# Three reorderings at the seam between attention and the feed-forward part: V's last transposes, one low part of W_ffn, one chunk of pair 2

## The chip, the cores and the metric

One core of one Trainium2 chip runs the whole kernel in one launch. The metric is device time in microseconds (us). The kernel before takes 1227.71 us, the median of 3 runs (1227.65 to 1227.83). The profiler took one further execution of its own, and all trace rows come from that one.

## The reference, cut to what matters

`x` is 32 sequences of 64 channels by 1024. A small network on `cond_128` mixes eight 64x64 matrices per sequence (`z` below), attention with 32 heads and a 10-row adapter prefix runs on the result, and its output projection is added to `x`. Then comes a grouped convolution of 9 taps, and a feed-forward layer (`W_base`, with a top-2 routed low-rank part) on its result.

```python
x = x + _L0_attn_ref(_L0_cond_ref(x, cond_128, ...), w_attn, w_proj, adapter_wte, gating)
x = x + _L0_ffn_ref(_L0_cond2_ref(x, cond_128, weight, c_weight, fside_S_0), W_base, b_base, W_router, A, B)
# in _L0_attn_ref:  y = softmax(q k^T / sqrt(hd), causal) v + gating * softmax(q ak^T / sqrt(C)) av;  return y w_proj^T
# in _L0_ffn_ref:   base = xf W_base^T + b_base;  logits = xf W_router^T;  lora = sum over the top 2 experts of w (xf A_e^T) B_e^T * 2
```

## The kernel before, in words

**Passes.** Every large product is made in three passes of a float32r high part and low part (high by high, high by low, low by high). ScalarE makes the high part by a copy, VectorE the low part by a subtraction, TensorE multiplies. So each weight and each activation must have gone through ScalarE and then VectorE before TensorE may use it.

**Attention stage.** The 2048 tokens stand as 4 units of 512 tokens, the 1024 columns as 8 groups of 128. The program goes through 32 units (g, u), numbered n. In `unit_step` TensorE projects K, Q and V of unit n (`project_qkv`, L803) and between these does the attention of unit n-1: scores (`attend_scores`, L755), V's transposes (`turn_values`, four transposes of vT into the PSUM bank bV, L810), the transposes of the probabilities (`attend_transposes`, L764 and L771) and the products with the values (`attend_values`, L780 and L786). ScalarE copies V out of PSUM (vT, L1060), and once it is transposed copies it into vbd (L1069, four copies).

**The seam.** The attention of the last unit, m = 31, has no projection of a further unit beside it. TensorE's program fills it with the first output projections: `project_out(p, c0, c1)` (L858) multiplies chunks c0 to c1 of the 8 chunks of pair p (2 sequences, 128 tokens); a chunk is three passes by two matmuls of 512 columns. Before its first chunk it waits for y_lo of pair p and, because all pairs accumulate into the same two banks bP, for x1_set of pair p-1, the residual of the pair before. `residual(p)` (L1209, VectorE) reads bP, adds x and writes x1.

VectorE's order there is a list written by hand (L1307 to L1320): the low part of y of pair 1 (`split_y(1)`, L1201), low parts of W_ffn (`wffn_lo(i)`, L1194, eight in all), residual(0), the softmax of unit 31 (L1148 to L1184), split_y(2), residual(1), `convolved(0)` (L1221 and L1227: the bias onto the convolution, then its low part clo), the rest of the low parts, the low part of the low-rank weights. ScalarE's order (L1076 to L1088) is unit 31's copies and exponentials, then split_y(1) (L1007), wffn_hi(0 to 3) (L1000), attend_exp(31), split_y(2), wffn_hi(4 to 6), attend_copies(31), y_copy(31), split_conv(0), wffn_hi(7). Here vbd's copies of unit 31 stand ahead of split_y(1), and they wait for V's transposes.

SyncE issues every transfer of the seam in one order: y and x of pair 0, W_ffn's blocks 0 and 1, y of pair 1; then (L682 to L694) W_ffn's blocks 2 to 6, y of pair 2, x1 of pair 0 to memory (`put_aside`), x of pair 1, and x1 back in eight strided pieces for the convolution (`spread`, L672). GpSimd makes x1b = x1 + bias (`add_bias`, L726); the first one waits for aprobs of unit 31, and residual(p+1) waits for x1b of pair p.

**Feed-forward stage.** For each of 16 pairs p (`pair_step`): the last layer of pair p (`last_layer`, L885, 8 chunks of 9 matmuls), some chunks of pair p+2's output projection, `turn_hidden` (L895, one transpose), some more chunks, `low_rank` (L905), `convolve(p+1)` (L870), and the remaining chunks. Beside these, VectorE does router(p) (L1241 to L1267), finish(p) (L1273, L1275), convolved(p+1) and residual(p+2). The chunk boundaries (c0, c1, c2) are (0, 3, 5) for all pairs but the first, where two chunks were already done after the first convolution.

Of the kernel before, what the change touches and what calls it, by code (L numbers as in the profile page):

```python
# [42 lines left out]
KC = L // P  # L43
# [20 lines left out]
def wait(eng, sem, value):  # L64

    if not isinstance(value, int) or value > 0:
        eng.wait_ge(sem, value)


def split_passes(hi_l, lo_l, hi_r, lo_r):  # L70

    return ((hi_l, hi_r), (hi_l, lo_r), (lo_l, hi_r))
# [286 lines left out]
def program(nc, d, psum, z, zbase, y_dram, x1_dram, ctx_dram, weights, out):  # L359
# [8 lines left out]
    with ExitStack() as ctx:  # L368
# [370 lines left out]
        def _(pe):  # L739
            mix_tensor(pe)  # L740
            def attend_scores(m, groups):

                pe.wait_ge(rotated[Q_], m + 1)
                pe.wait_ge(kbd_set, m + 1)
                wait(pe, aT_copied, m)
                wait(pe, pT_copied, 2 * m)
                wait(pe, ashifted, m)
                pe.wait_ge(akbd_set, groups)
                pe.wait_ge(avs_set, groups)
                for s in range(UP):  # L750
                    for b in range(2):
                        for t in range(2):
                            heads = slice(2 * HD * t, 2 * HD * (t + 1))
                            at = (s % 2) * SW
                            mm = pe.matmul(bS[2 * t + s // 2][NC * b:NC * b + NC, at:at + KW],  # L755
                                           qr[heads, (2 * s + b) * NC:(2 * s + b + 1) * NC],
                                           kbd[heads, 2 * s + b, :], start=True, stop=True)
                            if s == UP - 1 and b == 1:
                                mm.then_inc(scores, 1)
# [47 lines left out]
            def turn_values(m):  # L807
                pe.wait_ge(vT_copied, m + 1)
                for i in range(UP):
                    tr = pe.transpose(bV[:, i * P:(i + 1) * P], vT[:, i * P:(i + 1) * P], ident[:])  # L810
                tr.then_inc(v_tr, 1)
# [37 lines left out]
            def project_out(p, c0, c1):  # L849
                if c0 == 0:  # L850
                    pe.wait_ge(y_lo, p + 1)
                    wait(pe, x1_set, p)
                for c in range(c0, c1):
                    if p == 0:
                        pe.wait_ge(wp_lo, c + 1)
                    for i, (y, w) in enumerate(split_passes(*y_hi_lo[p], wphi, wplo)):
                        for n in range(2):
                            mm = pe.matmul(bP[:, n * 512:(n + 1) * 512], y[:, c, :], w[:, c, n * 512:(n + 1) * 512],  # L858
                                           start=(c == 0 and i == 0), stop=(c == KC - 1 and i == 2))
                if c1 == KC:  # L860
                    mm.then_inc(proj_mm, 1)

            def convolve(p):
                pe.wait_ge(x8_in, 16 * PH * (p + 1))
                wait(pe, conv_set, 2 * p)
                for b in range(2):
                    for g in range(CONV):
                        for j in range(2):
                            o = 512 * b + P * g
                            mm = pe.matmul(bC[:, o:o + P], x8[:, CONV * b + g, j:j + P], toep[:, g, j, :],  # L870
                                           start=(j == 0), stop=(j == 1))
                    mm.then_inc(conv_mm, 1)

            def last_layer(p, columns, c):

                if isinstance(p, int) and p == 0:
                    pe.wait_ge(wf_lo, c + 1)
                if c == 0:
                    pe.wait_ge(c_lo, 2 * (p + 1))
                for i, (a, w) in enumerate(split_passes(chi, clo, wfhi, wflo)):  # L880
                    for k in columns:
                        if c == 0 and i == 0:
                            wait(pe, bank_free[k], p)
                        at, n0, n1 = cuts[k]
                        mm = pe.matmul(bF[:, at:at + n1 - n0], a[:, c, :], w[c][:, n0:n1],  # L885
                                       start=(c == 0 and i == 0), stop=(c == KC - 1 and i == 2))
                        if c == KC - 1 and i == 2 and k == 2:
                            mm.then_inc(hidden_mm, 1)
                        if c == KC - 1 and i == 2 and k == 1:
                            mm.then_inc(ffn_mm, 1)  # L890

            def turn_hidden(p):
                pe.wait_ge(hw_set, p + 1)
                wait(pe, hwT_set, p)
                pe.transpose(bT[:, 0:P], hw[:], ident[:]).then_inc(hw_tr, 1)  # L895

            def low_rank(p):
                if isinstance(p, int) and p == 0:
                    pe.wait_ge(lora_lo, 1)
                pe.wait_ge(hwT_set, p + 1)  # L900
                for k in (2, 0, 1):
                    at, n0, n1 = cuts[k]
                    n1 = min(n1, L)
                    for h, w in split_passes(hwThi, hwTlo, loraBhi, loraBlo):
                        mm = pe.matmul(bF[:, at:at + n1 - n0], h[:], w[:, n0:n1],  # L905
                                       start=False, stop=True, skip_group_check=True)
                    if k != 0:
                        mm.then_inc(lora_mm, 1)
# [4 lines left out]
            m = NG * NU - 1  # L913
            pe.wait_ge(turned[Q_], NG * NU)
            pe.wait_ge(turned[K_], NG * NU)
            project_out(0, 0, KC)
            attend_scores(m, NG)
            turn_values(m)
            project_out(1, 0, 6)
            attend_transposes(m)  # L920
            project_out(1, 6, KC)
# [6 lines left out]
            def pair_step(p, ahead):  # L928
                if ahead >= 2:
                    for c in range(KC):  # L930
                        last_layer(p, (2, 0, 1), c)
                    c0, c1, c2 = (2, 5, 7) if p == 0 else (0, 3, 5)
                    project_out(p + 2, c0, c1)
                    if p == 0:
                        pe.wait_ge(y_copied, NG * NU)
                    turn_hidden(p)
                    project_out(p + 2, c1, c2)
                    low_rank(p)
                    convolve(p + 1)
                    project_out(p + 2, c2, KC)  # L940
                    return

                for k in (2, 0, 1):
                    if k == 1:
                        turn_hidden(p)
                    for c in range(KC):
                        last_layer(p, (k,), c)
                if ahead == 1:
                    convolve(p + 1)
                low_rank(p)  # L950

            for p in range(NP):
                pair_step(p, min(3, NP - 1 - p))
# [147 lines left out]
        def _(dve):  # L1101
# [90 lines left out]
            def wffn_lo(i):  # L1192
                dve.wait_ge(wf_hi_set, i + 1)
                dve.tensor_tensor(wflo[i][:], wf_raw[i][:], wfhi[i][:].bitcast(F32), ALU.subtract).then_inc(wf_lo, 1)  # L1194

            def split_y(p):
                dve.wait_ge(y_hi, p + 1)
                wait(dve, proj_mm, y_free(p))
                if p == 1:
                    dve.wait_ge(mm_done[V_], NU * NG)  # L1200
                dve.tensor_tensor(y_hi_lo[p][1][:], yst[:], y_hi_lo[p][0][:].bitcast(F32), ALU.subtract).then_inc(y_lo, 1)  # L1201
# [103 lines left out]
            for n in range(NG * NU):  # L1305
                unit_step(n // NU, n % NU)
            split_y(1)  # L1307
            for i in range(4):
                wffn_lo(i)
            residual(0)  # L1310
            attend_softmax(NG * NU - 1)
# [1 line left out]
            residual(1)  # L1313
            dve.wait_ge(fconsts, 16 * NFCONST)
            convolved(0)
            for i in range(4, KC):
                wffn_lo(i)
            dve.wait_ge(y_out, 16 * NG * NU)
            dve.wait_ge(lora_hi, 1)
# [113 lines left out]
```

## Time and profile before

| what | value |
|---|---|
| median of 3 runs | 1227.71 us |
| the profiled execution's own time | 1229.13 us |
| its span in the trace | 1226.6 us |
| PE busy | 1193.7 us (97%) |
| DVE busy | 736.8 us (60%) |
| ACT busy | 385.8 us (31%) |
| POOL busy | 79.2 us (6%) |
| share of PE in the chain that ended last | 93% |

PE is TensorE's matmuls, PEld its weight loads, DVE is VectorE, ACT ScalarE, POOL GpSimd, SPq SyncE's queue of transfers. Times in the trace are us from the span's start. In a timeline a row gives its start, its length, engine, line, operation, output and inputs, and the number of instructions; in brackets stands the engine's idle time before it and what ended that. Matmuls overlap, so the length of one is more than what it adds to the stream: the difference of two starts is what counts.

### The profile page before, as it was taken

To read this page: it belongs to the slowest core of one execution; us is meant where nothing else is said; L and a number is where in the kernel's file an instruction comes from. 1 tells how busy PE (TensorE), PEld (TensorE's weight loads), DVE (VectorE), ACT (ScalarE), POOL (GpSimd) and SP (SyncE) were. 2 spreads that over 40 slices of the span, in tenths; PEclk is the share of its full clock that TensorE was granted. 3 is DMA by queue.
4 is the path that set the end of the run, shared out by engine and by line. 5 is a ranking of instruction groups with operands and counts; after the bars stand their busy time and mean duration, and the time that the engine had idled before them with its cause. 6 is when DMAs were issued, how large, how long until landed. Compare 5 with 4: busy or idle time off the path is not lost.

```text
span 1226.6 us, 19491 instructions
## 1 busy us (share of the span) xinstructions
PE 1193.7 (97%) x7940; PEld 1036.6 (85%) x7940; DVE 736.8 (60%) x1489; ACT 385.8 (31%) x699; POOL 79.2 (6%) x41
## 2 busy tenths in 40 slices
PE   7899999999999999999999996999999999999998
PEld 6778888888888888888888885989999999999997
DVE  5966857767777768768577795533333333333332
ACT  4434443543535344344435462300100010110000
POOL 2700000000000000000000000100000111000001
PEclk9999999999999999999999998999999999999999
DMA  6311002001002002010020424422222232222221
GB/s 225 117 40 49 30 11 68 10 18 60 19 9 69 10 10 70 9 47 32 12 67 10 155 87 174 133 88 88 89 88 88 89 106 89 89 88 96 98 78 45
DMA packets 54917, 84.75 MB, mean 69 GB/s; under 512 B 5786, under 2 KB 41134, under 8 KB 53806
## 3 DMA queue, kind: packets, MB, share of 16 engines
q1 hardware_dynamic: 54830, 83.52, 20.2%
q8 instruction: 63, 1.03, 0.4%
q14 instruction: 24, 0.20, 0.1%
HBM read 58.33 MB, written 25.17 MB: 68 GB/s over the span
## 4 chain that ended last, share of the span: by engine, by line
PE 93%; DVE 4%; ACT 1%; issue 1%; DMA 0%; SPq 0%; DVEq 0%; ACTq 0%
PE psum L803 42%; PE psum L885 17%; PE psum L858 14%; PE psum L870 4%; PE psum L755 3%; PE psum L786 3%; PE psum L771 2%; PE psum L905 2%; PE psum L810 2%; DVE m_z L340 1%; DVE z L275 1%; PE psum L764 1%; PE psum L819 1%; PE psum L780 1%; DVE f_wflo L1194 0%
## 5 line engine op out<-in xcount | busy, mean ns | idle before, releaser
L803 PE MATMUL psum<-z,w_hi 128*128 128x512 f32 x1536 | 482.2, 395 | 3.6 <-DVE m_z L340 2.4
L803 PEld LDWEIGHTS psum<-z,w_hi 128*128 128x128 f32 x1536 | 283.7, 188 | 60.4 <-issue 2.6
L803 PE MATMUL psum<-z,w_lo 128*128 128x512 f32 x768 | 300.6, 391 | 0.0
L803 PEld LDWEIGHTS psum<-z,w_lo 128*128 128x128 f32 x768 | 144.5, 188 | 31.6
L1036 ACT ACTIVATE a_kbd<-a_kr 32x512 f32<-32x512 f32 x128 | 80.6, 630 | 225.5 <-DVE a_kr L1134 224.4
L726 POOL TENSOR_TENSOR f_x1b<-f_x,_bbase 128x1024 f32<-128x1024 f32 x16 | 49.3, 3079 | 1101.5 <-DVE a_aprob L1184 711.1
L885 PE MATMUL psum<-f_wfhi,f_chi 128*128 128x388 f32 (+1 forms) x384 | 94.5, 341 | 3.3 <-DVE f_clo L1227 1.8
L1148 DVE TENSOR_TENSOR a_prob<-psum,a_mask 128x512 f32<-128x512 f32 x64 | 44.0, 687 | 89.1 <-PE psum L755 89.1
L885 PE MATMUL psum<-f_wfhi,f_clo 128*128 128x388 f32 (+1 forms) x384 | 94.2, 340 | 0.0
L885 PE MATMUL psum<-f_wflo,f_chi 128*128 128x388 f32 (+1 forms) x384 | 94.2, 340 | 0.0
L1241 DVE COPY f_lg<-psum 128x8 f32<-128x8 f32 x16 | 2.7, 167 | 134.2 <-PE psum L885 134.2
L858 PE MATMUL psum<-f_wphi,f_yhi 128*128 128x512 f32 x240 | 77.1, 402 | 0.0
L858 PE MATMUL psum<-f_wplo,f_yhi 128*128 128x512 f32 x240 | 74.6, 392 | 0.0
L885 PEld LDWEIGHTS psum<-f_wfhi,f_chi 128*128 128x128 f32 x384 | 69.9, 189 | 5.3 <-DVE f_clo L1227 4.0
L858 PE MATMUL psum<-f_wphi,f_ylo 128*128 128x512 f32 x240 | 74.2, 390 | 0.0
L885 PEld LDWEIGHTS psum<-f_wfhi,f_clo 128*128 128x128 f32 x384 | 70.1, 189 | 0.0
L885 PEld LDWEIGHTS psum<-f_wflo,f_chi 128*128 128x128 f32 x384 | 69.8, 189 | 0.0
L1069 ACT ACTIVATE a_vbd<-psum 64x256 f32<-64x256 f32 x128 | 48.6, 380 | 45.7 <-PE psum L810 44.6
L1013 ACT ACTIVATE f_chi<-f_ct 128x512 fp32r<-128x512 f32 x32 | 20.2, 631 | 131.2 <-DVE f_ct L1221 131.2
L870 PE MATMUL psum<-_toep,_x 128*128 128x128 f32 x512 | 59.9, 275 | 0.0
L1018 ACT ACTIVATE f_rs<-f_rs 128x1 f32<-128x1 f32 x16 | 3.3, 203 | 179.1 <-DVE f_rs L1244 179.1
L870 PEld LDWEIGHTS psum<-_toep,_x 128*128 128x128 f32 x512 | 59.4, 192 | 0.1
(154 smaller groups left out, 1667.4 us busy)
## 6 DMA issues: line engine op xcount, KB each, us to landing
w_st<-in_wqkvT SPq DMA_DIRECT2D x8, 1536.0 KB, 7.2
m_x<-in_x SPq DMA_DIRECT2D x16, 512.0 KB, 4.3
y_scratch<-a_ysb SPq DMA_DIRECT2D x32, 256.0 KB, 2.5
f_yst<-y_scratch SPq DMA_DIRECT2D x16, 512.0 KB, 4.6
f_xt<-in_x SPq DMA_DIRECT2D x16, 512.0 KB, 3.9
x_scratch<-f_x SPq DMA_DIRECT2D x16, 512.0 KB, 2.6
_x<-x_scratch SPq DMA_DIRECT2D x128, 64.0 KB, 2.6
out<-f_osb SPq DMA_DIRECT2D x16, 512.0 KB, 2.7
```

The source lines that it names most:

```text
L726: pool.tensor_tensor(x1b[:].rearrange("p (m q) -> p q m", q=PH), x1[:].rearrange("p (q m) -> p q m", q=PH), bbase[:].rearrange("p (m q) -> ...
L755: mm = pe.matmul(bS[2 * t + s // 2][NC * b:NC * b + NC, at:at + KW], qr[heads, (2 * s + b) * NC:(2 * s + b + 1) * NC], kbd[heads, 2 * s + ...
L771: tr = pe.transpose(dst[:, j * P:(j + 1) * P], prob[t][:, 2 * j:2 * j + 2, :].rearrange("p h k -> p (h k)"), ident[:])
L786: mm = pe.matmul(y[2 * HD * hp:2 * HD * (hp + 1), (2 * s + b) * NC:(2 * s + b + 1) * NC], vbd[:, s, b, hp, :], pT[hp][:, s, NC * b:NC * b ...
L803: mm = pe.matmul(dst, w[:, c, x, :], zs, start=(c == 0 and i == 0), stop=(c == KC - 1 and i == 2))
L810: tr = pe.transpose(bV[:, i * P:(i + 1) * P], vT[:, i * P:(i + 1) * P], ident[:])
L858: mm = pe.matmul(bP[:, n * 512:(n + 1) * 512], y[:, c, :], w[:, c, n * 512:(n + 1) * 512], start=(c == 0 and i == 0), stop=(c == KC - 1 an ...
L870: mm = pe.matmul(bC[:, o:o + P], x8[:, CONV * b + g, j:j + P], toep[:, g, j, :], start=(j == 0), stop=(j == 1))
L885: mm = pe.matmul(bF[:, at:at + n1 - n0], a[:, c, :], w[c][:, n0:n1], start=(c == 0 and i == 0), stop=(c == KC - 1 and i == 2))
L1036: cp = act.activation(kbd[HD * h:HD * (h + 1), :, h % 2 * NC:(h % 2 + 1) * NC], kr[HD * h:HD * (h + 1), :].rearrange("p (b k) -> p b k", k ...
L1069: cp = act.activation(vbd[NC * h:NC * (h + 1), :, b, :, HD * h:HD * (h + 1)], bV[NC * b:NC * (b + 1), :].rearrange("p (s a h e) -> p s a h ...
L1148: dve.tensor_tensor(prob[t][:].rearrange("p (s h) k -> p s h k", h=2), score_slots[:, UP * t:UP * (t + 1), 0:2 * NC].rearrange("p s (h k) ...
```

## The change

Three edits of order; nothing is computed that was not computed before.

On TensorE, `turn_values(31)` goes ahead of `project_out(0, 0, KC)`; in the kernel before it stands behind both that and `attend_scores(31)`. On VectorE, three low parts of W_ffn instead of four go ahead of `residual(0)`, and the fourth (i = 3) goes to the head of those behind `convolved(0)`. On TensorE in pair 0, one of the two chunks of pair 2 that stood between `turn_hidden(0)` and `low_rank(0)` goes behind `convolve(1)`, where there was one chunk and are two now.

```diff
             pe.wait_ge(turned[K_], NG * NU)
+            turn_values(m)
             project_out(0, 0, KC)
             attend_scores(m, NG)
-            turn_values(m)
             project_out(1, 0, 6)
             attend_transposes(m)
             project_out(1, 6, KC)
...
-                    c0, c1, c2 = (2, 5, 7) if p == 0 else (0, 3, 5)
+                    c0, c1, c2 = (2, 5, 6) if p == 0 else (0, 3, 5)
                     project_out(p + 2, c0, c1)
...
             split_y(1)
-            for i in range(4):
+            for i in range(3):
                 wffn_lo(i)
             residual(0)
...
             convolved(0)
-            for i in range(4, KC):
+            for i in range(3, KC):
                 wffn_lo(i)
```

## Rows read from the trace of the kernel before

**Rows 1.** The page: TensorE's busy tenths in 40 slices of the span.
```profile
PE   7899999999999999999999996999999999999998
```

**Rows 2.** Waits of TensorE over the whole span (total, times, longest, us).
```profile
PE psum L858 <- DVE f_x L1209: 11.0, 1, 11.0
...
PE psum L885 <- DVE f_clo L1227: 1.8, 1, 1.8
```

**Rows 3.** The chain that ended last, 735 to 830 us (start, length, what).
```profile
739.01 11.11 PE psum L858 x48
...
751.28 0.60 PE psum L810 x4
...
760.90 1.82 DVE f_x L1209
```

**Rows 4.** Timeline of ScalarE: vT and vbd of unit 31.
```profile
737.73 0.60 ACT L1060 ACTIVATE a_vT<-psum 128x512 f32<-128x512 f32 x1 [1.57 <-PE psum L803]
...
751.91 1.55 ACT L1069 ACTIVATE a_vbd<-psum 64x256 f32<-64x256 f32 x4 [12.26 <-PE psum L810]
```

**Rows 5.** Timeline of VectorE at the seam.
```profile
755.71 5.19 DVE L1194 TENSOR_TENSOR f_wflo<-f_wf_raw,f_wfhi 128x1160 fp32r<-128x1160 f32 x4
...
772.14 0.24 DVE L1184 CAST a_aprob<-a_aprob 128x160 fp32r<-128x160 f32 x1
...
777.03 1.98 DVE L1209 TENSOR_TENSOR f_x<-psum,f_xt 128x1024 f32<-128x1024 f32 x1 [3.52 <-PE psum L858]
```

**Rows 6.** Timeline of TensorE at the seam.
```profile
762.85 1.19 PE L858 MATMUL psum<-f_wphi,f_yhi_next 128*128 128x512 f32 x2 [10.98 <-DVE f_x L1209]
...
772.72 0.60 PE L764 MATMUL psum<-_ident,a_aprob 128*128 128x128 f32 x4
```

**Rows 7.** Timeline of TensorE in pairs 0 and 1.
```profile
784.65 0.76 PE L885 MATMUL psum<-f_wfhi,f_chi 128*128 128x384 f32 x3
...
787.91 0.69 PE L885 MATMUL psum<-f_wfhi,f_chi 128*128 128x384 f32 x3
...
801.54 0.71 PE L858 MATMUL psum<-f_wphi,f_yhi 128*128 128x512 f32 x2
...
804.38 0.28 PE L905 MATMUL psum<-f_loraBhi,f_hwThi 128*128 128x248 f32 x1
...
812.67 0.80 PE L885 MATMUL psum<-f_wfhi,f_chi 128*128 128x384 f32 x3 [1.75 <-DVE f_clo L1227]
...
817.52 0.69 PE L885 MATMUL psum<-f_wfhi,f_chi 128*128 128x384 f32 x3
```

**Rows 8.** SyncE's queue and the landing of W_ffn's blocks (min, median, max).
```profile
740.09 3.05 SPq L614 DMA_DIRECT2D f_wf_raw<-in_wffnT  x5
...
DMA to landing us min/median/max: 4.2/6.5/9.3
```

**Rows 9.** Timeline of GpSimd: the first x1b.
```profile
772.46 4.08 POOL L726 TENSOR_TENSOR f_x1b<-f_x,_bbase 128x1024 f32<-128x1024 f32 x1 [711.13 <-DVE a_aprob L1184]
```

**Rows 10.** Timeline of VectorE: hwTlo of pair 0, and clo of pairs 1 and 2.
```profile
802.14 0.29 DVE L1267 TENSOR_TENSOR f_hwTlo<-psum,f_hwThi 128x128 fp32r<-128x128 f32 x1 [2.15 <-ACT f_hwThi L1021]
...
811.92 0.69 DVE L1227 TENSOR_TENSOR f_clo<-f_ct,f_chi 128x512 fp32r<-128x512 f32 x1 [0.70 <-ACT f_chi L1013]
...
841.56 0.69 DVE L1227 TENSOR_TENSOR f_clo<-f_ct,f_chi 128x512 fp32r<-128x512 f32 x1 [0.70 <-ACT f_chi L1013]
```

**Rows 11.** Stretches of 2 us: length, busy of PE, PEld, DVE, ACT, POOL, granted clock, DMA share, GB/s.
```profile
764.00:766.00 2.00, 2.00 (x7) 1.52 (x6) 1.96 (x3) 0.63 (x1) 0.00 (x0) 0.50 1.03 322
...
815.00:817.00 2.00, 2.00 (x8) 2.00 (x7) 0.58 (x1) 0.00 (x0) 0.00 (x0) 0.50 0.64 262
...
1208.00:1210.00 2.00, 1.94 (x11) 1.97 (x12) 0.79 (x1) 0.00 (x0) 1.07 (x1) 1.00 0.18 74
```

**Rows 12.** Timeline of TensorE: pair 2's last layer, and a wait near the end.
```profile
843.14 0.69 PE L885 MATMUL psum<-f_wfhi,f_chi 128*128 128x384 f32 x3
...
1208.06 0.41 PE L885 MATMUL psum<-f_wfhi,f_chi 128*128 128x384 f32 x1 [1.54 <-DVE f_osb L1273]
```

## The prediction

> **What bounds the kernel now.** I read the page's slices first: TensorE is busy at nine tenths or more nearly everywhere, and the one hole in the middle is the slice with a 6, at 736 to 767 us [rows 1]. So TensorE is the bound, and a change pays by what it takes out of TensorE's idle time or of its half-clock time. Second, the waits: one wait of 11.0 us of the first chunks of an output projection on the residual (DVE f_x L1209), and one of 1.8 us of the last layer on clo [rows 2]. Third, the chain and the timelines around the two, to see what ended last in each.
>
> At the first place, output projection 0 ends at 739.01 + 11.11 = 750.12, then the scores, then V's transposes, 0.60 long, at 751.28 [rows 3]. TensorE then has nothing until 762.85 [rows 6]. Pair 1's projection needs the banks that residual(0) frees, and residual(0) stands on VectorE behind split_y(1) and four low parts. split_y(1) needs ScalarE's high part, which stands behind vbd's copies, and these wait for V's transposes: vbd starts at 751.91 after 12.26 us of waiting [rows 4], the low parts start at 755.71 and take 5.19 [rows 5], and the residual runs from 760.90 for 1.82 [rows 3]. So in TensorE's order the transposes stand behind the very work whose end they hold up. The second place is 1.75 us at 812.67, where the last layer of pair 1 waits for clo [rows 7]; clo ends at 811.92 + 0.69 = 812.61 [rows 10].
>
> After each of the two the granted clock shows 0.50, the 1.2 GHz level: at 764 to 766 and at 815 to 817 [rows 11]. For the second its price can be read. The same six groups of three matmuls take 787.91 - 784.65 = 3.26 us in pair 0 and 817.52 - 812.67 = 4.85 in pair 1 [rows 7]: 1.59 us.
>
> **The change, part by part.**
>
> *V's transposes ahead.* They need vT, whose copy ends at 738.33 [rows 4], before TensorE is free at 739.01 [rows 3]; no wait is added. Four transposes are moved, no transfer with them. They put output projection 0 back by 0.60 us, so it ends at 750.72. ScalarE and VectorE then run vbd, split_y(1) and the low parts beside it. From vbd's start to the first low part's start was 755.71 - 751.91 = 3.80 us [rows 4, 5]; from about 739.7 that gives 743.5. Three low parts at 5.19 / 4 = 1.30 each [rows 5] end at 747.4 if their blocks have landed. That cover is output projection 0, and it has 3.3 us to spare.
>
> *Landing of W_ffn's blocks.* Block 2 is the first of five issued at 740.09, and landings take 4.2 to 9.3 us [rows 8]: between 744.3 and 749.4. In the worst case its high and low parts (1.3 us each, an estimate from the low part's row) end at 752.0 and residual(0) starts 1.3 us late. I take no delay, since the first of five should land nearer the short end, and keep 1.3 for the range. y of pair 2 is issued earlier too, behind these blocks; it is not needed until after unit 31's exponentials, 10 us on, and costs nothing.
>
> *One low part fewer ahead of residual(0).* By the sum above four would end at 748.7, still in time, so it is worth nothing alone, and 1.3 us only if block 3 is late. Behind convolved(0) it puts the four others and the low-rank low part back by 1.30. TensorE needs block 3 in the last layer's fourth chunk, three chunks (about 4.8 us) after its start at 784.65, while the low part of block 3 would be done 1.4 us after clo. Later blocks come every 1.3 us and are used every 1.6. Nothing.
>
> *What is late next.* Residual(0) starts at 750.76 and, at 1.90, ends at 752.66. TensorE starts pair 1 at about 752.8, where it was 762.85: 10.05 less. Its idle time there shrinks from 10.98 to about 0.9, because the scores end at 751.9. But unit 31's softmax still stands behind residual(0) on VectorE. It ended at 772.14 + 0.24 = 772.38 [rows 5], 9.66 after the residual's end at 762.72. So it will end at 752.66 + 9.66 = 762.32. TensorE needs six chunks before the transposes of the probabilities. At half clock at first it took 772.72 - 762.85 = 9.87 [rows 6]; at full clock a chunk is 1.38 (two chunks are 804.38 - 801.54 = 2.84, with some 0.09 of it a switch [rows 7]), six are 8.35, so it arrives at 761.2. A **new wait** of 1.2 us stands there, and the clock that is won back at this place is worth nothing. The transposes start at 762.4, where they were at 772.72: **10.3 us** in all.
>
> From there the order is as before. residual(1) waited for TensorE (3.52 idle), with x1b done at 772.46 + 4.08 = 776.54 and the residual started at 777.03 [rows 5, 9]; x1b hangs on the softmax like TensorE, so both move by about 10.3, and the half microsecond between them stays. spread(0) moves with residual(0) and stays ahead of the convolution.
>
> *The chunk of pair 2 behind the convolution.* low_rank(0) comes one chunk earlier: 804.38 - 1.38 = 803.0. It needs hwTlo, which ends at 802.43 [rows 10], 0.57 before; without that margin the gain would be cut by what is missing. The convolution, clo and the last layer of pair 1 follow it: clo at 812.61 - 1.38 = 811.23. TensorE now has two chunks (2.85) after a convolution ending at 809.28 - 1.38 = 807.9, so it arrives at 810.75 and waits 0.5 instead of 1.75. That is **1.38 us** saved in position (on top of the shift above).
>
> *The clock after it.* The trace has no wait of exactly 0.5 here. Bounds: the 1.75 us wait cost 1.59 more [rows 7], and a wait of 1.54 at 1208.06 [rows 12] was followed by a granted clock of 1.00 [rows 11]. 0.5 is nearer the latter, so I take the full **1.59 us** as saved, and 0 as the other end. The Trainium skill (TensorE: Matmul & The Clock Gate, the table under Why this matters for your kernels) gives a limit for idle gaps which a gap of 1.75 us does not reach. The trace disagrees, since the clock fell after just that gap. By the page the slow stretch would have another cause and stay, and the sum would be 1.59 less.
>
> **Sum:** 10.3 + 1.38 + 1.59 = 13.3 us. Against the profiled execution's 1229.13 that is 1215.8, a span of 1213.3. The profiled execution stands 1.42 above the median, and the same difference off the median gives 1227.71 - 13.3 = **1214.4**.
>
> **Rivals.**
> - *A: the clock falls at a new wait.* In the seam TensorE now waits twice, 0.9 and 1.2 us, and the second wait is followed by 1.2 us of transposes: 2.4 us without a full-width product, more than the 1.75 after which the clock fell. For it: that sum. Against: 1.54 held [rows 11, 12]. Price 1.59, on the path: 1216.0. The Trainium skill (same page, PE-mode transpose) says that transposes don't count as busy for the clock in the way matmuls do; by that this case is the one to expect. No row here separates it.
> - *B: the slow stretch in pair 1 stays,* by a phase of the clock rather than by the gap's length: 1216.0.
> - *C: block 2 lands late,* 1.3 us on residual(0) and all behind it: 1215.7.
> - *D: slower.* In pairs 2 to 13 TensorE reaches the last layer 0.9 us after clo (841.56 + 0.69 = 842.25 against 843.14 [rows 10, 12]). If the shift upset the order of VectorE and GpSimd there so that clo came more than 0.9 later, each pair would stall and might run at half clock. With the price of pair 1, up to 1.75 + 1.59 = 3.34 in each of 12 pairs, 40 us: 1254. It decides the sign at 1.1 us per pair. Against: what these pairs wait for is all relative to TensorE itself, and nothing in them is edited.
> - *E: the moved transposes don't free split_y(1),* because y of pair 1 or something else was late too. Then only the low part moved away (1.3) and the chunk (2.97) count: 1223.4. Against: ScalarE's 12.26 us are put down to the transposes, and nothing idles between vbd and the low parts.
>
> **How the numbers follow.** The forecast has 0.6, A 0.14, B 0.10, C 0.08, E 0.04, D 0.02, and 0.02 is left for others. The range reaches below by 1.4 for errors of the terms and of the comparison with the median, and above to A and C or A and B together (1217.6). 0.2% is 2.5 us, about what a measurement of this kernel can tell from no change. All but D and the rest lie more than that below 1227.7: faster 0.97, same 0.01, slower 0.02.
>
> **What would show it.** Right: TensorE's L858 wait on f_x drops from 11.0 to about 0.9; vbd starts near 739.7; a new wait of about 1.2 on a_aprob before L764 at about 762.4; pair 1's wait on clo at 0.5; clock 1.00 throughout the seam. Wrong: low parts idling for wfhi beyond 750.7 (C), a clock of 0.50 after 762 (A) or in pair 1's last layer (B), waits on clo in pairs 2 to 13 (D), ScalarE idle behind vbd (E).

## The result, and the profile after

| | before | after |
|---|---|---|
| median | 1227.77 us (1227.65 to 1228.57, 4 runs) | 1215.65 us (1215.03 to 1215.94, 4 runs) |
| ratio | | 0.9899, 95% interval 0.9882 to 0.9916 |
| profiled execution, its span | 1229.13, 1226.6 | 1215.03, 1212.7 |

The change takes 12.1 us off, 1.0%. The forecast was 1214.4 in a range of 1213.0 to 1217.6. The interval of the ratio reaches from 10.3 to 14.5 us off, so the times alone do not tell 12.1 from the 13.3 of the sum; what follows on the single terms rests on the traces. The slice that read 6 in TensorE's row [rows 1] reads 9 now:

```profile
PE   7899999999999999999999999999999999999998
```

The waits of TensorE over the whole span of the changed kernel (total, times, longest):

```profile
PE psum L764 <- DVE a_aprob L1184: 1.0, 1, 1.0
PE psum L858 <- DVE f_x L1209: 0.9, 1, 0.9
...
PE psum L885 <- DVE f_clo L1227: 0.4, 1, 0.4
```

The 11.0 us have become 0.9 and the 1.8 have become 0.4 [rows 2], and a wait that was not there before, 1.0 on aprob, has come in. The timeline of TensorE in the changed kernel puts them in order:

```profile
737.30 1.15 PE L786 MATMUL psum<-a_pT,a_vbd 128*64 128x64 f32 x32
738.38 0.66 PE L810 MATMUL psum<-_ident,a_vT 128*128 128x128 f32 x4
...
752.07 0.70 PE L858 MATMUL psum<-f_wphi,f_yhi_next 128*128 128x512 f32 x2 [0.94 <-DVE f_x L1209]
...
761.63 0.66 PE L764 MATMUL psum<-_ident,a_aprob 128*128 128x128 f32 x4 [1.00 <-DVE a_aprob L1184]
...
791.96 0.28 PE L905 MATMUL psum<-f_loraBhi,f_hwThi 128*128 128x248 f32 x1
...
800.32 0.79 PE L885 MATMUL psum<-f_wfhi,f_chi 128*128 128x384 f32 x3 [0.44 <-DVE f_clo L1227]
```

V's transposes now stand directly behind the products with the values. ScalarE no longer waits 12 us for them, and VectorE, which began the residual 10.78 us after the end of projection 0 (760.90 against 750.12 [rows 3]), is now idle 3.20 us before it. Here are ScalarE's and then VectorE's timeline of the changed kernel:

```profile
739.07 1.55 ACT L1069 ACTIVATE a_vbd<-psum 64x256 f32<-64x256 f32 x4
```

```profile
742.88 3.91 DVE L1194 TENSOR_TENSOR f_wflo<-f_wf_raw,f_wfhi 128x1160 fp32r<-128x1160 f32 x3
750.00 1.92 DVE L1209 TENSOR_TENSOR f_x<-psum,f_xt 128x1024 f32<-128x1024 f32 x1 [3.20 <-PE psum L858]
...
761.34 0.24 DVE L1184 CAST a_aprob<-a_aprob 128x160 fp32r<-128x160 f32 x1
```

The residual starts when projection 0 ends. The softmax ends 761.58 - 751.92 = 9.66 us after the residual, as it did before, and TensorE is there 1.00 us too early. The granted clock stays at 1.00 behind each of the three waits, on f_x, on aprob and on clo, as three stretches of 2 us of the changed kernel show (same columns as [rows 11]):

```profile
752.00:754.00 2.00, 1.93 (x9) 1.62 (x10) 1.93 (x4) 0.08 (x1) 0.00 (x0) 1.00 0.67 242
...
762.00:764.00 2.00, 2.00 (x16) 1.82 (x15) 0.71 (x1) 1.58 (x3) 2.00 (x1) 1.00 0.00 0
...
801.00:803.00 2.00, 2.00 (x13) 2.00 (x12) 2.00 (x2) 0.04 (x1) 0.00 (x0) 1.00 0.00 0
```

One thing has to be taken out before spans are compared. The start of unit 30's products with the values (L786), the last work ahead of all edits, lay between 736.94 and 738.22 us in the executions profiled for this study. That is scatter of an unedited part. So below stands, beside the times, **the stretch**: from that start to the end of the span. It is 1226.6 - 737.85 = 488.75 us in the first profile of before (its L786 row is in the experiment on the kernel before) and 1212.7 - 737.30 = 475.40 after: 13.35 less, where the sum said 13.3. Spans are given to 0.1 us, so a stretch is no finer than that.

### The profile page after: what moved, and what is told of

It reads as the page before. It is cut to its first block, busy times and chain, and to the rows that moved or that the text cites. A ratio compares the mean times of both kernels' runs of the same rounds, so it can differ in the third digit from the quotient of the medians.

```text
span 1212.7 us, 19491 instructions
## 1 busy us (share of the span) xinstructions
PE 1191.8 (98%) x7940; PEld 1034.2 (85%) x7940; DVE 736.6 (61%) x1489; ACT 386.0 (32%) x699; POOL 79.1 (7%) x41
## 4 chain that ended last, share of the span: by engine, by line
PE 93%; DVE 5%; ACT 1%; issue 1%; DMA 0%; SPq 0%; DVEq 0%; ACTq 0%
PE psum L803 42%; PE psum L885 17%; PE psum L858 14%; PE psum L870 4%; PE psum L755 3%; PE psum L786 3%; PE psum L771 2%; PE psum L905 2%; PE psum L810 2%; DVE m_z L340 1%; DVE z L275 1%; PE psum L764 1%; PE psum L819 1%; PE psum L780 1%; PE psum L205 0%
```

## The experiments

The first four put single parts of the change on the kernel before. All ran on one chip, beside 21 runs of before with a median of 1228.17 (1227.00 to 1229.42).

**V's transposes alone.**

```diff
+            turn_values(m)
             project_out(0, 0, KC)
             attend_scores(m, NG)
-            turn_values(m)
```

> V's transposes ahead of output projection 0, and nothing else of the change. Theory (the transposes alone held up the seam, and the softmax of unit 31 is late next): residual(0) starts when output projection 0 ends, since four low parts end before it too; 10.3 us less than the kernel before, about 1217.4. The wait on clo in pair 1 stays at 1.75 and the clock falls behind it. Rival (the low part taken away is needed as well): residual(0) starts about 1.3 us after projection 0's end, 9.0 us less, about 1218.7.

Measured: 1217.01 (1216.73 to 1217.29), ratio 0.9911 (0.9896 to 0.9926), stretch 476.67. TensorE's timeline of this run:

```profile
752.39 0.70 PE L858 MATMUL psum<-f_wphi,f_yhi_next 128*128 128x512 f32 x2 [0.94 <-DVE f_x L1209]
...
801.93 0.79 PE L885 MATMUL psum<-f_wfhi,f_chi 128*128 128x384 f32 x3 [1.72 <-DVE f_clo L1227]
...
805.22 0.69 PE L885 MATMUL psum<-f_wfhi,f_chi 128*128 128x384 f32 x3
```

The theory holds: the wait is 0.94 with four low parts too. But one thing came out otherwise. Behind the wait of 1.72 on clo the first six groups of the last layer take 805.22 - 801.93 = 3.29 us, the full-speed price. The clock did not fall, against the expectation.

**The low part alone.**

```diff
-            for i in range(4):
+            for i in range(3):
                 wffn_lo(i)
...
-            for i in range(4, KC):
+            for i in range(3, KC):
                 wffn_lo(i)
```

> Three low parts of W_ffn instead of four ahead of residual(0), and nothing else of the change. Theory (VectorE's list is the path of the seam once the transposes are late): residual(0) starts 1.3 us earlier, TensorE's wait on it falls from 11.0 to 9.7, 1.3 us less in all, about 1226.4. Rival (the low parts are beside the path, ScalarE's copies carry it): no change, 1227.7.

Measured: 1226.84 (1226.12 to 1227.48, 11 runs), ratio 0.9990 (0.9981 to 0.9999), which is 1.3 us. Its timeline of TensorE:

```profile
761.15 1.19 PE L858 MATMUL psum<-f_wphi,f_yhi_next 128*128 128x512 f32 x2 [9.70 <-DVE f_x L1209]
...
771.47 0.60 PE L764 MATMUL psum<-_ident,a_aprob 128*128 128x128 f32 x4
...
811.40 0.80 PE L885 MATMUL psum<-f_wfhi,f_chi 128*128 128x384 f32 x3 [1.74 <-DVE f_clo L1227]
```

The wait went from 10.98 to 9.70: while the transposes are late, the low part taken away was on the path. The rival is out. Here too the clock did not fall behind the wait of 1.74: the six groups of the last layer behind it ran at a granted clock of 1.00.

**The chunk alone.**

```diff
-                    c0, c1, c2 = (2, 5, 7) if p == 0 else (0, 3, 5)
+                    c0, c1, c2 = (2, 5, 6) if p == 0 else (0, 3, 5)
```

> One chunk of pair 2 behind the convolution, and nothing else of the change. Theory (position 1.38, and the granted clock no longer falls, 1.59): the wait on clo in pair 1 falls from 1.75 to about 0.4, the granted clock stays at 1.00 there, 3.0 us less in all, about 1224.8. Rival (the clock's fall has another cause): a granted clock of 0.50 stays in pair 1's last layer, 1.4 us less, about 1226.3.

Measured: 1226.64 (1225.48 to 1227.28, 11 runs), ratio 0.9989 (0.9980 to 0.9998): 1.5 us less, half of what the theory wanted, and yet not by the rival's mechanism. Its timeline of TensorE:

```profile
762.69 1.19 PE L858 MATMUL psum<-f_wphi,f_yhi_next 128*128 128x512 f32 x2 [10.97 <-DVE f_x L1209]
...
773.42 0.60 PE L764 MATMUL psum<-_ident,a_aprob 128*128 128x128 f32 x4
...
811.97 0.79 PE L885 MATMUL psum<-f_wfhi,f_chi 128*128 128x384 f32 x3 [0.35 <-DVE f_clo L1227]
...
815.26 0.69 PE L885 MATMUL psum<-f_wfhi,f_chi 128*128 128x384 f32 x3
```

The wait on clo is 0.35 and the six groups behind it take 3.29 us at full speed, as the theory wants. What is odd lies at the first place: the six chunks of pair 1 behind the 11 us wait took 773.42 - 762.69 = 10.73 us, where the first profile of before had 9.87 [rows 6]. So the time at half clock varied between executions, and the theory's base was one of them. The stretch bears this out: it is 1224.3 - 737.70 = 486.60, which is 2.15 below the first profile of before, and 3.01 below it once the 0.86 more at the first place is taken out.

**The change without its edit on VectorE.**

```diff
-            for i in range(3):
+            for i in range(4):
                 wffn_lo(i)
...
-            for i in range(3, KC):
+            for i in range(4, KC):
                 wffn_lo(i)
```

> The change without its edit on VectorE: four low parts ahead of residual(0). Theory (hidden behind output projection 0): the fourth low part ends about 1.9 us before projection 0 does, TensorE's wait on f_x stays at 0.9, the time is that of the change within its scatter, 13.3 us below before. Rival (needed once the transposes are early): 1.3 us more than the change.

Measured: 1215.34 (1214.73 to 1215.62), ratio 0.9897 (0.9882 to 0.9912), stretch 475.38 against 475.40 of the change. VectorE's timeline of this run shows the cover:

```profile
742.91 5.30 DVE L1194 TENSOR_TENSOR f_wflo<-f_wf_raw,f_wfhi 128x1160 fp32r<-128x1160 f32 x4
750.02 1.92 DVE L1209 TENSOR_TENSOR f_x<-psum,f_xt 128x1024 f32<-128x1024 f32 x1 [1.80 <-PE psum L858]
```

Even with the fourth low part VectorE is idle 1.80 us before the residual. The edit is worth 1.3 us alone and nothing beside the transposes.

**The kernel before, twice more.** No edit; this is the run that the odd rows asked for.

> The kernel before, unedited, for a second profiled execution. In the first the granted clock fell to 0.50 behind the wait of 1.75 in pair 1; in the runs with one part of the change alone it did not fall behind a wait of 1.72 and of 1.74. Theory (a wait of that length brings the clock down in some executions and not in others, so the 1.59 is counted in full only against the one profiled execution): the wait is 1.7 to 1.8 again, and the last layer's first six groups take either 3.3 or about 4.9 us. Rival (the fall belongs to the kernel before and is there in each execution): 4.9 here and in the next.

> The kernel before, unedited, for a third profiled execution; as the one before it. By the theory at least one of the two shows 3.3 us for the six groups and a granted clock of 1.00 there; by the rival neither does. The time of TensorE's six chunks of pair 1 behind the 11 us wait, 9.87 in the first profile and 10.73 in the run with the chunk alone, should vary as well, between about 9.7 and 10.7.

Measured: 1228.93 and 1226.78, each a single profiled execution. For comparison, the row of the first profile of before from which its stretch is counted:

```profile
737.85 1.15 PE L786 MATMUL psum<-a_pT,a_vbd 128*64 128x64 f32 x32
```

The timeline of TensorE in the second execution of before, then in the third:

```profile
737.69 1.15 PE L786 MATMUL psum<-a_pT,a_vbd 128*64 128x64 f32 x32
...
812.56 0.79 PE L885 MATMUL psum<-f_wfhi,f_chi 128*128 128x384 f32 x3 [1.81 <-DVE f_clo L1227]
...
817.38 0.69 PE L885 MATMUL psum<-f_wfhi,f_chi 128*128 128x384 f32 x3
```

```profile
737.23 1.15 PE L786 MATMUL psum<-a_pT,a_vbd 128*64 128x64 f32 x32
...
762.22 1.19 PE L858 MATMUL psum<-f_wphi,f_yhi_next 128*128 128x512 f32 x2 [10.98 <-DVE f_x L1209]
...
771.98 0.60 PE L764 MATMUL psum<-_ident,a_aprob 128*128 128x128 f32 x4
...
811.89 0.80 PE L885 MATMUL psum<-f_wfhi,f_chi 128*128 128x384 f32 x3 [1.74 <-DVE f_clo L1227]
...
815.18 0.69 PE L885 MATMUL psum<-f_wfhi,f_chi 128*128 128x384 f32 x3
```

A stretch of 2 us behind that wait, in the second and in the third execution:

```profile
814.00:816.00 2.00, 2.00 (x7) 2.00 (x7) 1.45 (x2) 0.00 (x0) 0.00 (x0) 0.50 0.39 158
```

```profile
813.00:815.00 2.00, 2.00 (x13) 2.00 (x12) 1.81 (x2) 0.00 (x0) 0.00 (x0) 1.00 0.22 88
```

The same program and the same wait: six groups in 4.82 us where the granted clock shows 0.50, and in 3.29 us where it stays at 1.00. The stretches are 1226.5 - 737.69 = 488.81 and 1224.3 - 737.23 = 487.07. So the 1.59 us belong to some executions of before and not to others; the rival, a fall in each, is out. How many have it is not shown. Nine runs of before on the same chip lie at 1228.27 to 1229.51, all nearer the second execution than the third, so there the fall may well be the common case.

The rest are edits of the changed kernel. The first three of them ran beside one more measurement of the changed kernel itself, on another chip than the runs above.

**The change once more.** No edit.

> The changed kernel once more, unedited, as the measure for the three beside it. By the forecast 13.3 us below before (1214.4); by the first measurement 12.1 (1215.65). Theory (the difference of 1.2 is scatter of the unedited first 60 us, where the clock falls in some phase): TensorE reaches the last unit's products with the values (L786) at a time that varies by up to 1 us between executions, and the stretch from there to the end is 13.3 us shorter than before. Rival (the clock falls at a new wait in some executions): the stretch from there to the end itself is longer by about 1.6 in this one.

Measured: 1215.43 (1215.37 to 1215.65), ratio 0.9896 (0.9881 to 0.9911), stretch 1213.0 - 737.62 = 475.38. The stretch is the same as in the first profile, 475.40, and the granted clock is 1.00 behind both new waits in each, so the rival did not come. Against before's 488.75 the theory's 13.3 holds, against the 487.07 of the third execution it is 11.7. So the 1.2 us that this expectation puts down to the opening can also be before's own scatter at half clock; no run splits them between the two.

**No chunk behind the convolution.**

```diff
-                    c0, c1, c2 = (2, 5, 6) if p == 0 else (0, 3, 5)
+                    c0, c1, c2 = (2, 5, 8) if p == 0 else (0, 3, 5)
...
-                    project_out(p + 2, c2, KC)
+                    if c2 < KC:
+                        project_out(p + 2, c2, KC)
```

> The changed kernel with no chunk of pair 2 behind the convolution: both stand between the transpose and the low-rank product of pair 0. Theory (a long enough wait brings the clock to half): the wait on clo in pair 1 grows from 0.44 by two chunks plus what low_rank(0) is later, to about 3.2; the last layer of pair 1 starts 2.8 us later than in the changed kernel, and the granted clock falls behind it, some 1.6 us more: 4.4 us above the changed kernel. Rival (the clock's fall in the kernel before was not due to the wait): 2.8 us above.

Measured: 1219.88 (1219.76 to 1220.04), 4.45 above the changed kernel, stretch 1217.5 - 737.93 = 479.57, 4.2 above. Its timeline of TensorE:

```profile
803.54 0.79 PE L885 MATMUL psum<-f_wfhi,f_chi 128*128 128x384 f32 x3 [3.07 <-DVE f_clo L1228]
...
808.36 0.69 PE L885 MATMUL psum<-f_wfhi,f_chi 128*128 128x384 f32 x3
```

Behind a wait of 3.07 the six groups take 4.82 us. All five runs lie within 0.3 us, so the fall probably came in each of them. The theory's two terms are both there: the last layer of pair 1 starts 65.61 us after L786 instead of 63.02, which is 2.6 (2.8 expected), and the six groups take 1.5 more (1.6 expected).

**Three chunks behind the convolution.**

```diff
-                    c0, c1, c2 = (2, 5, 6) if p == 0 else (0, 3, 5)
+                    c0, c1, c2 = (2, 4, 5) if p == 0 else (0, 3, 5)
```

> The changed kernel with pair 0's transpose of hw one chunk earlier, and three chunks of pair 2 behind the convolution instead of two. Theory (the wait on clo, 0.44, is all that is left there): low_rank(0) starts 1.38 earlier, clo with it, TensorE has three chunks of cover, no wait, 0.4 us less than the changed kernel. Rival (hw or hwTlo is late, one chunk is too little cover for it): TensorE waits up to 1 us at the transpose or at low_rank(0) and nothing is won, or up to 0.6 is lost.

Measured: 1215.14 (1214.66 to 1215.40), 0.3 below the changed kernel, with ranges that touch; stretch 1212.9 - 738.22 = 474.68, 0.7 below. The wait on clo is gone and none has come at the transpose or at the low-rank product. The theory's 0.4 lies between the two.

**Both waits filled.**

```diff
-            project_out(1, 0, 6)
+            project_out(1, 0, 7)
             attend_transposes(m)
-            project_out(1, 6, KC)
+            project_out(1, 7, KC)
...
-                    c0, c1, c2 = (2, 5, 6) if p == 0 else (0, 3, 5)
+                    c0, c1, c2 = (2, 4, 5) if p == 0 else (0, 3, 5)
```

> As the run with three chunks behind the convolution, and seven chunks of pair 1 instead of six ahead of unit 31's transposes of the probabilities. Theory (TensorE waits 1.0 us there for the softmax with work at hand that it could do): the wait disappears, the transposes start 0.4 later, and one chunk stands behind them instead of two; 1.0 us less there, 1.4 less than the changed kernel. Rival (with one chunk as cover, ScalarE's copies of the transposed probabilities, 1.7 us, become late): up to 0.5 of it comes back as a wait before the products with the values.

Measured: 1213.81 (1212.70 to 1214.04), ratio 0.9883 (0.9868 to 0.9898), 1.6 below the changed kernel beside it, with no overlap of the two ranges; stretch 1210.4 - 736.94 = 473.46, 1.9 below. This is the lowest median of all. Its timeline of TensorE, and then of VectorE:

```profile
761.50 0.60 PE L764 MATMUL psum<-_ident,a_aprob 128*128 128x128 f32 x4
...
764.53 1.15 PE L786 MATMUL psum<-a_pT,a_vbd 128*64 128x64 f32 x32
```

```profile
765.48 1.96 DVE L1209 TENSOR_TENSOR f_x<-psum,f_xt 128x1024 f32<-128x1024 f32 x1 [3.13 <-POOL f_x1b L726]
```

No wait is left at the transposes or ahead of the products with the values. What is late next shows on VectorE: residual(1) now waits for GpSimd's x1b, where it had waited for TensorE [rows 5].

**The seventh chunk alone,** on the changed kernel; its diff is the first part of the one above. This run and the next ran beside before's runs on a chip of their own (median 1228.54).

> The changed kernel with seven chunks of pair 1 ahead of unit 31's transposes of the probabilities, and nothing else. Theory (the new wait of 1.0 us behind the softmax can be filled by the seventh chunk): no wait at the transposes, 1.0 us less than the changed kernel, about 1214.4. Rival (it was the chunk moved in pair 0 that brought most of the run with both, 1.6): 0.4 less at most.

Measured: 1214.26 (1213.62 to 1214.58), ratio 0.9881 (0.9866 to 0.9896); stretch 1212.2 - 738.05 = 474.15, 1.25 below the changed kernel's. The changed kernel itself was not run on that chip. The transposes start 0.24 us later than in the changed kernel (762.62 - 738.05 against 761.63 - 737.30), and one chunk less stands behind them. The rival allowed 0.4. Filling the wait of 1.0 brings most of what the run with both brings.

**The transposes in the middle of projection 0.**

```diff
-            turn_values(m)
-            project_out(0, 0, KC)
+            project_out(0, 0, 4)
+            turn_values(m)
+            project_out(0, 4, KC)
```

> The changed kernel with V's transposes behind four chunks of output projection 0 instead of ahead of it, 5.5 us later. Theory (VectorE sat idle 3.2 us before residual(0) in the changed kernel, and that is all the slack the chain from the transposes has): the residual starts 5.5 - 3.2 = 2.3 us later, TensorE's wait on it grows from 0.9 to about 3.2, and the time by 2.3 to 3.2, the more where the clock falls behind the wait: 1217.8 to 1218.7. Rival (the chain is shorter or longer than the rows say, since ScalarE waited 0.5 for a block of W_ffn too): 1.8, since that wait is absorbed as well.

Measured: 1218.03 (1217.78 to 1219.15), ratio 0.9917 (0.9903 to 0.9930); stretch 1215.4 - 737.83 = 477.57, 2.2 above the changed kernel. Its timelines of TensorE and VectorE, and the stretch behind the wait:

```profile
754.80 0.70 PE L858 MATMUL psum<-f_wphi,f_yhi_next 128*128 128x512 f32 x2 [3.05 <-DVE f_x L1210]
```

```profile
752.77 1.88 DVE L1210 TENSOR_TENSOR f_x<-psum,f_xt 128x1024 f32<-128x1024 f32 x1
```

```profile
755.00:757.00 2.00, 2.00 (x10) 1.61 (x10) 1.93 (x4) 0.35 (x1) 0.00 (x0) 1.00 0.77 264
```

The residual starts 752.77 - 737.83 = 14.94 us after L786, where it was 750.00 - 737.30 = 12.70: 2.24 later, so the slack was the 3.2 us of the theory. The rival counted on ScalarE's wait of 0.54 for a block of W_ffn; that wait stands behind the three copies that the residual needs, off the path. And behind a wait of 3.05 the granted clock stays at 1.00 in this execution. One of the five runs, the one of 1219.15, had a mean granted clock of 0.995 where the others had 0.997 or 0.998; no trace shows where it fell.

## Why the prediction was right

- **The bound, and V's transposes** (10.3). Right, and in the place named: residual(0) starts with the end of projection 0, TensorE's wait is 0.94 (0.9 forecast), and the stretch of the run with the transposes alone is 487.07 - 476.67 = 10.4 below that execution of before which, like it, had no half clock in pair 1. The 10.3 hold what the half clock after the 11 us wait cost in the first profile (9.87 us for six chunks); with the 9.76 and 10.73 of other executions it would be 10.2 and 11.2. The cover of 3.3 us is 3.20, and the transposes in the middle show what happens once it is used up.
- **One low part fewer.** Right: nothing beside the transposes. Without them it is worth 1.3 us, as the size of one low part says.
- **What is late next.** Right: the softmax, 9.66 us behind the residual. The new wait is 1.00, where 1.2 was forecast.
- **The chunk** (1.38). Right in position: the wait is 0.44 (0.5 forecast), and low_rank(0) found hwTlo ready (VectorE had it done at 791.37, 0.59 before). The change's stretch is 11.67 below the third execution of before, which is 10.3 + 1.38.
- **The clock after it** (1.59). Mis-sized. The step took one execution's price for the price of the kernel. In three profiles of before the fall came twice (4.85 and 4.82 us) and was absent once (3.29), and it was absent with the transposes alone and with the low part alone (after waits of 1.72 and 1.74). So the step that failed is taking it as certain: its worth to a median is the 1.59 times the share of executions that have it, and that share is not known. Three measurements of the transposes with the chunk against before, on three chips, gave 12.1, 12.6 and 12.8 us less (the last without the edit on VectorE). They lie between the 11.7 without this term and the 13.3 with all of it, though each has some 2 us of uncertainty.
- **From the profiled execution to the median.** Here the same error may have come in a second time. The sum against the profiled execution's own 1229.13 gave 1215.8, and the changed kernel ran in 1215.03 to 1215.94. The text then took 1.42 off for how far that execution stood above the median. But it can have stood there because it held the 1.59, which the sum had already taken out: the third execution, without the fall, took 1226.78. This is argued from single executions. Without that subtraction the forecast would have been 1215.8, which is 0.15 from what was measured instead of 1.25; within the scatter of 0.9 that is no proof of it.
- **Rivals.** A (a fall at a new wait) did not come in the two profiles of the changed kernel: the granted clock is 1.00 behind the wait of 1.00 and the transposes. So nothing in them bears out the part that the prediction gave to the Trainium skill's sentence on transposes (TensorE: Matmul & The Clock Gate, PE-mode transpose). They do not test that sentence itself either, since no run varies the transposes behind a wait. B (the slow stretch stays) is out for the wait of 0.4. C (a late block) is out, since VectorE was idle 3.20 us. D and E did not happen: the only waits of TensorE behind the seam are the 0.44 and one of 1.5 near the end, as before.
- **What the Trainium skill says of idle gaps** (TensorE: Matmul & The Clock Gate, the table under Why this matters for your kernels). A gap of 1.75 does not reach the limit that it gives, and the clock fell there in two executions of three. No limit on the gap's length alone fits these runs: 1.75 and 1.81 were followed by a fall, 1.74 and 3.05 were not, 3.07 was.

What stays open is how often before's clock falls in pair 1, and what decides it. The 21 runs of before on one chip spread over 2.4 us and the times alone don't tell a fall from the scatter of the opening.

## What to carry to other kernels

Where the bound engine waits long for a chain over two other engines, look for the small step of its own that feeds that chain, and issue it ahead of the big block that is to cover the chain. Then look at once for what is late next: here a wait of 1.0 us behind the softmax, filled by one more chunk for 1.2 us. And a term read off one profiled execution, above all half-clock time behind a wait (here of 1.75 to 3.07 us), needs a second profile of the same kernel; whoever removes such a term must not also take off the execution's distance from the median.

## What the runs showed of the hardware that was not expected

After an unchanged wait of 1.74 to 1.81 us the same program ran on at a granted clock of 0.50 in two executions and at 1.00 in a third, 1.5 us apart. The length of the half-clock time after the 11 us wait varied too: the same six chunks took 9.76 us in the third execution of before (762.22 to 771.98), 9.87 in the first and 10.73 in the run with the chunk alone. The changed kernel, which has no wait over 1.0 us there, stayed within 0.9 us in its first measurement and 0.3 in its second, and before's 21 runs on one chip within 2.4; but with 4 runs against 21 that does not show that the half-clock time is the cause.

The opening, which no run edits, shows the same in all fourteen profiles. There TensorE waits 2.41 to 2.43 us for VectorE's z at about 51.5 us. The clock fell behind that wait in ten profiles. In the other four it did not; TensorE then waited 2.69 to 2.74 us at the next place, where the ten waited 1.11 to 1.16, and the clock fell behind that. Here is the first wait with the stretch behind it in the first profile of before, then the same two lines and the next wait in the run with the transposes alone:

```profile
51.22 0.70 PE L803 MATMUL psum<-z,w_hi 128*128 128x512 f32 x2 [2.42 <-DVE m_z L340]
...
53.00:55.00 2.00, 2.00 (x6) 1.52 (x6) 2.00 (x4) 1.06 (x1) 1.07 (x2) 0.50 0.00 0
```

```profile
51.48 0.70 PE L803 MATMUL psum<-z,w_hi 128*128 128x512 f32 x2 [2.42 <-DVE m_z L340]
...
53.00:55.00 2.00, 2.00 (x11) 1.65 (x10) 2.00 (x5) 1.06 (x1) 1.07 (x2) 1.00 0.00 0
...
59.91 0.73 PE L803 MATMUL psum<-z,w_hi 128*128 128x512 f32 x2 [2.74 <-DVE w_lo L326]
```

So one wait of the same length, behind the same work, was followed by either level of the clock.
